# Float32 products of unsplit operands in the expert blocks of a mixture-of-experts layer, in place of three float32r terms

## The reference

```
xt = layernorm(x).reshape(1024, 256)
logits = xt @ Wr.T + bias;  two highest of softmax(logits) per row, weights w normalised
g = einsum('th,ehi->tei', xt, Wg);  u = einsum('th,ehi->tei', xt, Wu)   # E = 16 experts, i = 128
y = einsum('tei,eih->teh', silu(g) * u, Wd)
routed = sum over the two chosen experts of w * y
shared = (silu(xt @ sWg) * (xt @ sWu)) @ sWd
x = x + 0.5 * (routed + shared)
```

## Time and profile before

| | us |
|---|---|
| median of 3 timed runs | 350.92 |
| lowest and highest | 347.88, 352.57 |
| span of the profiled execution | 375.8 |
| TensorE products busy in it | 276.6 |
| VectorE busy | 244.9 |
| ScalarE busy | 167.1 |
| GpSimd busy | 130.5 |

### The profile page before, as it was taken

One profiled execution on the slowest core, in us unless ns is written; L12 is line 12 of the kernel. 1 busy time (PEld: TensorE's weight loads), 2 busy tenths in 40 slices (PEclk: granted clock), 3 DMA queues, 4 the chain that ended last, 5 costly groups with the idle time before them and its releaser, 6 DMA issues.

```text
span 375.8 us, 6430 instructions
## 1 busy us (share of the span) xinstructions
PE 276.6 (74%) x1911; PEld 199.4 (53%) x1911; DVE 244.9 (65%) x800; ACT 167.1 (44%) x433; POOL 130.5 (35%) x181
## 2 busy tenths in 40 slices
PE   1747649888882587989999999987384598898710
PEld 1537428877771254555444444654273287787700
DVE  8686865757666871658888885466841266667616
ACT  3566604434443155357666666662321044444300
POOL 7027841555456003300445200000077125555630
PEclk9966757999997799898999999999696599999965
DMA  7996654434400617980534400000022603344127
GB/s 249 385 388 191 261 161 161 120 99 130 131 19 15 210 42 185 197 250 26 113 88 85 86 3 1 2 3 0 0 101 98 195 15 110 108 138 131 31 81 254
DMA packets 29861, 45.69 MB, mean 122 GB/s; under 512 B 5323, under 2 KB 22961, under 8 KB 29444
## 3 DMA queue, kind: packets, MB, share of 16 engines
q1 hardware_dynamic: 24164, 33.41, 29.2%
q0 software_dynamic: 5664, 11.87, 10.9%
HBM read 27.98 MB, written 20.61 MB: 129 GB/s over the span
## 4 chain that ended last, share of the span: by engine, by line
PE 54%; DVE 19%; issue 7%; DMA 7%; ACT 7%; POOL 2%; another core or an unknown queue 2%; SPq 1%; POOLq 0%; DVEq 0%; ACTq 0%
PE bank L313 23%; PE bank L1015 5%; PE bank L1054 5%; PE bank L1028 4%; PE bank L320 4%; PE bank L947 4%; PE bank L871 3%; DVE wl L1212 3%; DMA yg<-results 2%; DVE res L1384 2%; PE bank L1032 2%; DMA stk_q<-parts_d 1%; DVE xn L1227 1%; PE bank L856 1%
## 5 line engine op out<-in xcount | busy, mean ns | idle before, releaser
L568 POOL DMA_INDIRECT results<-ysb,xp x62 | 61.5, 993 | 75.4 <-DVE ysb L1351 55.6
L1440 DVE CUSTOM_DVE_ANT_0 bank<-bank,dec 128x512 f32<-128x512 f32 (+3 forms) x128 | 59.8, 518 | 18.2 <-PE bank L1015 18.0
L1312 DVE TENSOR_TENSOR hm<-sg,bank 128x128 f32<-128x128 f32 x78 | 22.3, 286 | 51.4 <-ACT sg L654 30.7
L820 ACT ACTIVATE ct<-bank 128x512 f32<-128x512 f32 (+1 forms) x96 | 45.0, 520 | 22.0 <-PE bank L1032 21.9
L654 ACT ACTIVATE sg<-bank 128x128 f32<-128x128 f32 x78 | 21.5, 276 | 63.8 <-PE bank L313 54.4
L557 POOL DMA_INDIRECT slots_x<-xn,slot x32 | 34.1, 1064 | 33.3 <-DVE slot L1289 24.3
L313 PE MATMUL bank<-wh,xT_h 128*128 x124 | 41.3, 333 | 3.7 <-DVE xT_l L1339 2.9
L700 ACT ACTIVATE xT_h<-bank 128x256 fp32r<-128x256 f32 x62 | 23.8, 386 | 34.7 <-PE bank L947 30.6
L871 PE MATMUL bank<-ident,hm 128*128 128x128 f32 x78 | 23.7, 304 | 20.4 <-issue 11.3
L1015 PE MATMUL bank<-stk_q,stk_k 96*128 96x512 bf16 (+3 forms) x128 | 34.9, 310 | 2.1 <-DMA stk_q<-parts_d 1.8
L313 PE MATMUL bank<-wh,hT_h 128*128 (+1 forms) x78 | 30.7, 394 | 7.2 <-issue 2.7
(11 more groups left out here) (186 smaller groups left out, 681.5 us busy)
## 6 DMA issues: line engine op xcount, KB each, us to landing
xp<-slots_x SPq DMA_DIRECT2D x30, 257.0 KB
w_raw<-in_experts SPq DMA_DIRECT2D x17, 384.0 KB, 8.4
yg<-results SPq DMA_DIRECT2D x16, 256.0 KB, 4.8
slots_x<-zeros SPq DMA_DIRECT2D x2, 1285.0 KB, 11.8
parts_d<-part SPq DMA_DIRECT2D x6, 384.0 KB, 3.2
stk_k<-parts_d SPq DMA_DIRECT2D x8, 192.0 KB, 3.8
stk_q<-parts_d POOLq DMA_DIRECT2D x8, 192.0 KB, 4.9
slots_x<-zeros SPq DMA_DIRECT2D x1, 1413.5 KB, 7.8
```

Source lines behind the costliest of these rows:

```text
L568: pool.indirect_dma_start(results, where, ysb[c % RING][:], None, bounds_check=4 * N - 1, oob_is_err=False).then_inc(s_ys[c % RING], 16)
L820: act.activation(ct[n % 6][:, a:b], bank[2 + i][:, 0:b - a], ACT.Exp).then_inc(s_exp, 1)
L1440: dve.tensor_tensor_reduce(s_i, s_i, dec[:, SEQ - w:SEQ], 1.0, NEG, ALU.add, ALU.max, mmax[g % 2][:, n % G * QT + i:n % G * QT + i + 1])\
```

## The change

In the expert blocks, rows and weights are no longer split. `w_raw` keeps all raw experts in memory of its own, and TensorE multiplies float32 by float32: two products for gate and up, one for down. ScalarE still copies the turned rows and hidden rows, now as float32 (`xT`, `hE`); VectorE's two subtractions per block go. Only the shared expert's weights are split (`whl_s`), and its rows and hidden rows stay split as well. The waits on low parts (`s_xtl`, `s_htl`) become waits on the copies (`s_xth`, `s_hth`), and TensorE waits for all sixteen raw experts (`s_w`) ahead of the blocks of pass 0.

```
-        xT = [[sb(f"xT{j}_{i}", [P, KT, P], F32R, r2) for i in "hl"] for j in range(2)]
+        xT = [sb(f"xT{j}", [P, KT, P], F32, r2) for j in range(2)]
+        hE = [sb(f"hE{j}", [P, P], F32, r2) for j in range(2)]
...
-                if f == 0:
-                    for q in (1, 2):
-                        split_high(q)
...
-                    if f == 0 and EARLY + i <= E:
-                        split_high(EARLY + i)
...
                     if live[2]:
-                        hidden_high(j - 2, j % 2, False)
+                        act.wait_ge(s_ht, j - 1)
+                        act.wait_ge(s_y, j - 3)
+                        act.activation(hE[j % 2][:], bank[4 + j % 2][:, 0:P], ACT.Copy).then_inc(s_hth, 1)
...
                 if f == 0:
-                    pe.wait_ge(s_wlo_v, E + 1)
-
-                whl = [w[:].rearrange("p e n -> p (e n)") for w in (wh, wl)]
+                    for q in range(1, E + 1):
+                        pe.wait_ge(s_w[q], 16)
+
+                w_all = w_raw[:].rearrange("p e n -> p (e n)")
...
                     if live[1]:
-                        pe.wait_ge(s_xtl, n)
-                        gate_up(j - 1, (j - 1) % 2, b - 1 >= 2, lambda k, a: xT[(b - 1) % 2][a][:, k, :],
-                                lambda k, c: whl[c][:, bass.ds(at[b - 1] + k * GU, GU)])
+                        pe.wait_ge(s_xth, n)
+                        if b - 1 >= 2:
+                            pe.wait_ge(s_hm, j - 2)
+                        for k in range(KT):
+                            mm = pe.matmul(bank[2 + (j - 1) % 2][:, 0:GU], xT[(b - 1) % 2][:, k, :],
+                                           w_all[:, bass.ds(at[b - 1] + k * GU, GU)], start=k == 0, stop=k == KT - 1)
+                        mm.then_inc(s_gu, 1)
...
                     if live[3]:
+                        pe.wait_ge(s_hth, j - 2)
                         if f or b >= 5:
                             pe.wait_ge(s_ye, n - 4)
-                        down(j - 3, (j - 3) % 2, lambda c: whl[c][:, bass.ds(at[b - 3] + KT * GU, D)])
+                        pe.matmul(bank[6 + (j - 3) % 2][:, 0:D], hE[(j - 3) % 2][:],
+                                  w_all[:, bass.ds(at[b - 3] + KT * GU, D)], start=True, stop=True).then_inc(s_y, 1)
...
-                    if f == 0:
-                        for q in (i + 1,) if i < 6 else (2 * i - 5, 2 * i - 4):
-                            split_low(q)
...
-                    if live[0]:
-                        dve.wait_ge(s_xth, f * NB + b + 1)
-                        dve.tensor_tensor(xT[b % 2][1][:], bank[b % 2][:, 0:D].rearrange("p (k t) -> p k t", k=KT),
-                                          xT[b % 2][0][:].bitcast(F32), ALU.subtract).then_inc(s_xtl, 1)
...
-                    if live[2]:
-                        hidden_low(j - 2, j % 2)
```

More of the change, by code:

```diff
@@ L72, in macaron_kernel @@
         bank = [ctx.enter_context(nc.psum_tensor(f"bank{i}", [P, 512], F32)) for i in range(8)]
[L75 to L79, removed]
+        w_raw = sb("w_raw", [P, E + 1, WE])
+        whl_s = [sb(f"ws_{i}", [P, WE], F32R) for i in "hl"]
         rw = [sb(f"rw_{i}", [P, KT, E], F32R) for i in "hl"]
@@ L238, in macaron_kernel @@
         s_xth = sem("s_xth")
-        s_xtl = sem("s_xtl")
         s_gu = sem("s_gu")
@@ L631, in load_table, with split_high @@
                 loads[0] += 1
-            def split_high(q):
-                act.wait_ge(s_w[q], 16)
-                act.activation(wh[:, order[q], :], w_raw[:, order[q], :], ACT.Copy).then_inc(s_whi, 1)
+            def split_high():
+                act.wait_ge(s_w[0], 16)
+                act.activation(whl_s[0][:], w_raw[:, E, :], ACT.Copy).then_inc(s_whi, 1)
             def deviation(n, r):
@@ L678, in ffn @@
                 load_table(ACT.Silu)
-                if f == 0:
-                    for q in range(3, EARLY):
-                        split_high(q)
                 for i in range(NT + 2):
@@ L699, in step @@
                             act.wait_ge(s_gu, j - 1)
-                        act.activation(xT[b % 2][0][:], bank[b % 2][:, 0:D].rearrange("p (k t) -> p k t", k=KT),
+                        act.activation(xT[b % 2][:], bank[b % 2][:, 0:D].rearrange("p (k t) -> p k t", k=KT),
                                        ACT.Copy).then_inc(s_xth, 1)
@@ L724, in _ @@
                     turn_high(0, r - 2)
-            split_high(0)
+            split_high()
             logits_out(0, 0)
@@ L865, in gate_up, with hidden_turn, down @@
                 three(pe, bank[2 + par][:, 0:GU], xs, ws, None).then_inc(s_gu, 1)
-            def hidden_turn(j, par, first):
+            def hidden_turn(j, par, low):
                 pe.wait_ge(s_hm, j + 1)
-                if not first:
-                    pe.wait_ge(s_htl, j - 1)
+                if j >= 2:
+                    pe.wait_ge(s_hth, j - 1)
+                if low:
+                    pe.wait_ge(s_htl, low)
                 pe.transpose(bank[4 + par][:, 0:P], hm[par][:], ident[:]).then_inc(s_ht, 1)
-            def down(j, par, wd):
-                pe.wait_ge(s_htl, j + 1)
+            def down(j, par, low, wd):
+                pe.wait_ge(s_htl, low)
                 three(pe, bank[6 + par][:, 0:D], lambda k, a: hT[par][a][:], lambda k, b: wd(b),
@@ L912, in w_s @@
                 def w_s(k, b):
-                    return (wh, wl)[b][:, E, k * GU:(k + 1) * GU]
+                    return whl_s[b][:, k * GU:(k + 1) * GU]
                 for i in range(NT + 2):
@@ L919, in ffn @@
                     if 0 <= i - 1 < NT:
-                        hidden_turn(j - 1, (j - 1) % 2, f == 0 and i - 1 < 2)
+                        hidden_turn(j - 1, (j - 1) % 2, f * NT + i - 2 if i >= 3 else 0)
                     if 0 <= i - 2 < NT:
@@ L923, in ffn @@
                             pe.wait_ge(s_ysh, f * NT + i - 3)
-                        down(j - 2, j % 2, lambda b: (wh, wl)[b][:, E, KT * GU:WE])
+                        down(j - 2, j % 2, f * NT + i - 1, lambda b: whl_s[b][:, KT * GU:WE])
                 pe.wait_ge(s_ysh, (f + 1) * NT)
                 if f == 0:
-                    pe.wait_ge(s_wlo_v, E + 1)
-                whl = [w[:].rearrange("p e n -> p (e n)") for w in (wh, wl)]
+                    for q in range(1, E + 1):
+                        pe.wait_ge(s_w[q], 16)
+                w_all = w_raw[:].rearrange("p e n -> p (e n)")
                 at = {}
@@ L944, in step @@
                         if b < 2 and f:
-                            pe.wait_ge(s_xtl, n - 1)
+                            pe.wait_ge(s_xth, n - 1)
                         for k in range(KT):
@@ L950, in step @@
                     if live[1]:
-                        pe.wait_ge(s_xtl, n)
-                        gate_up(j - 1, (j - 1) % 2, b - 1 >= 2, lambda k, a: xT[(b - 1) % 2][a][:, k, :],
-                                lambda k, c: whl[c][:, bass.ds(at[b - 1] + k * GU, GU)])
+                        pe.wait_ge(s_xth, n)
[5 more added lines that the diff above has]
+                        mm.then_inc(s_gu, 1)
                     if live[2]:
-                        hidden_turn(j - 2, j % 2, b - 2 >= 2)
+                        hidden_turn(j - 2, j % 2, 0)
                     if live[3]:
+                        pe.wait_ge(s_hth, j - 2)
                         if f or b >= 5:
                             pe.wait_ge(s_ye, n - 4)
-                        down(j - 3, (j - 3) % 2, lambda c: whl[c][:, bass.ds(at[b - 3] + KT * GU, D)])
+                        pe.matmul(bank[6 + (j - 3) % 2][:, 0:D], hE[(j - 3) % 2][:],
+                                  w_all[:, bass.ds(at[b - 3] + KT * GU, D)], start=True, stop=True).then_inc(s_y, 1)
                 over_blocks(step)
@@ L1207, in link, with split_low @@
                 dve.wait_ge(s_dv, steps[0])
[L1209 to L1212, removed]
+            def split_low():
+                dve.wait_ge(s_whi, 1)
+                dve.tensor_tensor(whl_s[1][:], w_raw[:, E, :], whl_s[0][:].bitcast(F32), ALU.subtract)\
                     .then_inc(s_wlo_v, 1)
@@ L1406, in _ @@
                     router_low()
-            split_low(0)
+            split_low()
             ffn(0)
```

1 line of the change is left out of this document (removed).

## The result

| us | before | changed | ratio, 95% interval |
|---|---|---|---|
| first measurement, medians | 351.75 | 355.91 | 1.0215 (1.0137 to 1.0293) |
| second measurement, other chip | 349.88 | 356.86 | 1.0188 (1.0132 to 1.0244) |

The ratios are those on record and not the quotients of the medians, which are 1.012 and 1.020. Both intervals exclude 1, so the changed kernel is slower; whether by more than 2% they leave undecided. By the medians the change costs 4 to 7 us, by the ratios 6.6 to 7.6; 14 were forecast, and 365 us was predicted against 355.9 measured. The median of before has one execution more than the table ahead of the prediction. The profiled execution of the changed kernel took 358.18 us with a span of 356.4, 1.8 us around it.

What follows compares the result with a forecast made beforehand. TensorE was taken as the bound, VectorE a close second. Block products +17.7, half clock +1.5, ends -1.5 and weight split -3.2 gave +14.5 us on 350.9: 365 us, own range 358 to 373, 8 in 10 for 351 to 374.

Steps and rivals of the forecast that it cites:

- rival A: Expert blocks: timed blocks already near 1.8 us for a cause outside TensorE, so the new 1.67 us hides; 350 us, 15%.
- The sign: Whole kernel: slower by 4%, with TensorE the bound of the blocks; 75% for slower by over 2%.
- The stalls: Expert blocks and pass 1's late start: the profiled execution's 24.9 us over the median are stalls absent from timed runs.
- my two sums: Profiled stalls: 22 us in blocks above 1.38 us plus 3.1 us late start of pass 1, together 25 us.
- C: Expert blocks: stalls are real, caused by close VectorE-TensorE hand-overs, and vanish with VectorE halved; 342 us, 5%.
- B: Block products: each float32 product costs its constant every time, 0.56 us; 387 us, 9%.
- D: Block products: float32 runs as one instruction of one step a column, leaving GpSimd's 1.28 us floor; 340 us, 2%.
- The product: Block products: one float32 product of 256 columns taken at 0.44 us, ends 0.43 and 0.56.
- The block before: Expert blocks of the kernel before: period 1.38 us in a timed run, twelve TensorE instructions of 0.115 us.
- The first blocks: First blocks of each pass: full +0.285 us per block, plus +1.5 us (0 to 3) more at half clock.
- Part 3: Ahead of pass 0's blocks: weight split gone, earlier first turn and shorter row scatters; -3.2 us (0 to -4.0).
- The ends: Ends of both passes: shorter VectorE chain and less scatter queue against longer last products; -1.5 us (-2.5 to 0).

Runs made afterwards that it cites:

- e4: Kernel before with the fourth term, low part by low part, added to each block product; 368.71 us, ratio 1.0479.
- e3: Changed kernel with the down product of each block issued twice, the second overwriting the first; 380.52 us, ratio 1.0863.
- e2: Changed kernel with VectorE's two subtractions per block put back into spare tiles, TensorE waiting for them as before; 360.30 us, ratio 1.0269.
- before_again: Kernel before, no edit, profiled once more; 350.87 us, ratio 1.0024, span 349.2 us.
- v2: Changed kernel with the long filler in pass 1 alone, 40 products ahead of the scatter wait and 12 behind; 355.76 us, ratio 1.0159.
- v3: Kernel before with pass 0's six filler products ahead of the last weight-split wait, and the long filler in pass 1; 349.57 us, ratio 0.9937.
- after_again: Changed kernel, no edit, run once more; 356.86 us, ratio 1.0188, span 354.5 us.
- e1: Changed kernel with the sixteen expert weight splits put back at their old places, results unread, TensorE's old wait kept; 360.54 us, ratio 1.0259.
- e5: Kernel before without the term rows' low part by weights' high part, and without VectorE's two subtractions per block; 340.58 us, ratio 0.9681.
- e6: Kernel before without the term rows' low part by weights' high part, VectorE's two subtractions and their waits kept; 345.58 us, ratio 0.9818.
- e7: Changed kernel with the long filler in both passes, 40 products ahead of the scatter wait and 12 behind; 358.64 us, ratio 1.0204.
- v1: Kernel before with 20 (pass 0) and 40 (pass 1) filler products ahead of the waits, 5 and 12 behind; 352.14 us, ratio 1.0077.

## Why the prediction was right, and where its sizes were not

**The total: right in sign, and inside the wide range by luck.** The forecast of 365 us had a range of its own, 358 to 373 us, and both medians, 355.9 and 356.9, lie below it. They lie inside the 351 to 374 us given for 8 in 10 because that range was widened for part of rival A, and rival A, whose own 345 to 356 us the first median falls into, did not happen. The chance of 75% for slower by over 2% is neither borne out nor refuted by 1.9 and 2.2%.

**The sign, and its reason: right.** TensorE was the bound of a timed block before (e4) and is now (no idle in 42.3 us, e3). The three float32 products cost more than the nine they replace, and VectorE's relief pays nothing in the middle of a pass (e2).

**The stalls: right that a timed run has none, on weak grounds.** The argument was the gap of 24.9 us between span and median. before_again shows the undisturbed execution with a span of 349.2 us. That my two sums met at 25 us was partly chance: against before_again the 26.6 us between the spans are 20.3 in the 52 steps, 5.9 between the passes, and 0.4 in all the rest. The thought recorded with e2, that the number of instructions or hand-overs per block might cause them, got no support (e4). Rivals A and C needed them in timed runs and fall; B falls with 0.43 us per product; D was never near.

**The product, 0.44 taken, 0.427 measured.** The lower end, four clock steps a column at 2.4 GHz, is the value: 6x0.2133 + 3x0.115 = 1.625 us, measured 1.627. The constant of 0.12 us in the earlier trace rows is not paid in a stream.

**The block before, 1.38 taken, 1.409 measured.** I read the period off three undisturbed blocks of the earlier trace rows. The usual step of before_again is 1.395 us, and one late step in each pass is 0.36 us longer. With the product this makes +0.219 us per block instead of +0.285: over the 52 measured steps 11.4 us instead of 14.8.

**The first blocks: the step that failed.** I charged the full difference per block there and +1.5 us more for the half clock. Measured is -3.2 us for the first four of each pass. Two things are in it. At full clock the four take about the same time in both kernels, 4.72 and 4.93 us (v2, v3), with TensorE busy 4.4 and 4.1 of it. The changed kernel has one VectorE step less ahead of the first product, and TensorE waits less for it (v2, then v3):

```profile
286.80 1.13 PE L951 MATMUL bank<-w_raw,xT 128*128 x4 [0.34 <-ACT xT L689]
```

```profile
284.94 0.38 PE L313 MATMUL bank<-wh,xT_h 128*128 x1 [0.80 <-DVE xT_l L1341]
```

That much is shown, and the 0.46 us between the two are near the 0.42 us that I had looked for at this end of a pass. The rest is when the clock rose. In before_again it was at half nearly throughout (0.56 and 0.57 granted), in after_again 0.96 and 0.78. But the changed kernel's first profile had it at half up to 5.3 us after the first turn of pass 1, and the four blocks then took 7.0 us. And in the first profile of the kernel before it rose only 0.3 us after the first turn of pass 1. So in pass 1 it may have been the moment at which it happened to rise. In pass 0 it rose 0.1 to 0.4 us after the first turn in the changed kernel's two profiles and in v2, but 1.0 and 3.0 us after it in e2 and e3; with the splits it took 0.6 to 6.2 us (before, before_again, e1, e4, e5, e6). The timed runs speak for a real effect: their granted clocks are 0.861 to 0.891 in 52 runs of the kernel before (one of 629 us left out) and 0.880 to 0.902 in ten of the changed one. As an estimate from clock and span, that is 93 against 78 us at half clock in the median. How much of it lies in the first blocks the timed runs don't show. So the share of the change in these 2 to 3 us stays open.

**Part 3, -3.2 taken, -4.0 measured** (-3.7 to -4.6 by e1 against the changed kernel's medians, -1.5 to -2.5 against its ratios). Here the upper end of what I had worked out was reached: the first load landed 2.7 us after its issue instead of the 3.5 assumed, and the long scatters are gone. From the start of the first row scatter to the end of the last it is 23.5 us in before_again and 20.8 in after_again, the 2.6 us that the scatters gain; the end of the wait for the split gives the rest. The rule of the Trainium skill (page SBUF — State Buffer, opening part on the two sides) on instructions that exclude each other is borne out as far as the runs go: maximum scatter 1657 and 1743 ns with the splits, 1249 without, and 1748 again in e1. The scatters of before_again that take longer than in the changed kernel, by 0.3 us or more, are four, and each starts while a weight subtraction runs.

**The ends, -1.5 taken, 0 measured at the last blocks.** From the last row turn to the last result scatter it is 7.1 us in before_again and 7.05 in after_again, and the same in pass 1. The longer last products seem to eat up the shorter chain, but no run separates the two. What the shorter chain gives at the start of a pass is counted with the first blocks.

**Sum.** Predicted +17.7 + 1.5 - 1.5 - 3.2 = +14.5. Measured in the two spans: +11.4 - 3.2 - 4.0 + 1.1 = +5.3.

## What to carry to other kernels

A float32 product in place of split terms should be priced in time on TensorE: here 0.427 us for one against 0.345 for three terms, so it is a loss where TensorE is the bound, as here, and a gain only by what the splitting holds up elsewhere, here 4 us before the first block of one pass. A steady-state difference per block should not be applied to the blocks that fill the pipeline. And where a profiled span is far above the timed runs, profile the same kernel again before reading periods from it.

## What the runs showed of the hardware

- One recorded execution had 20 us of stalls in its 52 steps: about every third step took 2.1 to 3.4 us, where 1.40 is usual, while later executions of the same program and of larger ones had none. Its means per stretch misled by 27%, 1.79 against 1.41 us; an undisturbed stretch gave the period good to 2%.
- VectorE's four steps, 1.41 us by their single durations, passed in a period of 1.355 us (e6): here the sum of durations overstates what the engine needs.
- From the start of the six filler products to the full clock it took 8.6 us in both passes of before_again, but 3.1 and 5.2 us in after_again, 2.8 and 8.2 us in the changed kernel's first profile, and 8.7 and 2.9 us in that of the kernel before. With a filler of 52 products that ran up to the first turn the clock was at full there in all five places where it was put (e7 in both passes; v1, v2 and v3 in pass 1).
- Four row scatters of pass 0 that began while VectorE ran a weight subtraction of 0.95 us took 1.29 to 1.66 us in before_again, where the same four take 0.97 in the changed kernel.
